# Layer 2 of the late blocks: half in parts, half plain, with the row moves, row loads and transposes reordered

## The reference, cut to what matters

```python
x = x + L0_xattn_ref(ctx_1024, _layernorm(x), ...)          # attention, 32 batches
def _L0_ffn_ref(...):                                        # D = 256, F = 1024, 8 experts
    assign = argmax(x @ centroids.T)                         # one expert for each token
    xn  = layer_norm(x) * ln_g[e] + ln_b[e]
    h   = relu(xn @ w1[e].T + b1[e])                         # layer 1: 256 -> 1024
    y   = x + h @ w2[e].T + b2[e]                            # layer 2: 1024 -> 256
    out = alpha * y + (1 - alpha) * x                        # alpha = sigmoid(x . centroid)
x = x + _L0_ffn_ref(_layernorm(x), ...)
```

## Time and profile before

| | us |
|---|---|
| median of 3 runs | 1070.32 (1070.15 to 1070.99) |
| the profiled execution | 1066.71 |
| its span | 1064.9 |
| TensorE matmul busy | 1051.3 (99%) |
| VectorE busy | 796.3 (75%) |
| ScalarE busy | 670.9 (63%) |
| GpSimd busy | 494.8 (46%) |

### The profile page before, as it was taken

The page is one execution under the profiler, slowest core; times in us unless marked ns, Lnnn a source line. Parts: engine busy times, 40 slices in busy tenths (PEclk is TensorE's granted clock), DMA queues, the critical chain, the costliest instruction groups (busy, mean ns, idle before and its releaser), DMA issues.

```text
span 1064.9 us, 24086 instructions
## 1 busy us (share of the span) xinstructions
PE 1051.3 (99%) x8454; PEld 941.1 (88%) x8454; DVE 796.3 (75%) x1907; ACT 670.9 (63%) x1820; POOL 494.8 (46%) x647
## 2 busy tenths in 40 slices
PE   8989999999999999999999999999999999999998
PEld 6879898988888888989898888888898999999997
DVE  7867888888888988888888888898886554544441
ACT  6765757585676766575757567676555646656551
POOL 2744464646454555546464645455445342222222
PEclk9999999999999999999999999999999999999999
DMA  6576667585757676766658575766367657767670
GB/s 209 120 194 148 165 166 189 139 218 139 207 144 185 150 194 163 188 161 174 181 146 213 145 206 139 190 149 157 90 170 226 236 196 249 240 223 232 227 260 28
DMA packets 159660, 190.51 MB, mean 179 GB/s; under 512 B 17453, under 2 KB 149037, under 8 KB 154672
## 3 DMA queue, kind: packets, MB, share of 16 engines
q1 hardware_dynamic: 155088, 179.09, 61.6%
q0 software_dynamic: 3360, 8.53, 2.2%
q10 hardware_dynamic: 1088, 1.31, 0.4%
HBM read 65.72 MB, written 46.07 MB: 105 GB/s over the span
## 4 chain that ended last, share of the span: by engine, by line
PE 94%; POOL 2%; DVE 2%; DMA 1%; issue 1%; ACT 0%; SPq 0%; POOLq 0%; DVEq 0%
PE psum L698 17%; PE psum L731 16%; PE psum L873 12%; PE psum L768 11%; PE psum L858 10%; PE psum L747 9%; PE psum L783 9%; PE psum L717 8%; PE psum L786 1%; POOL prob L1701 1%; POOL w_o_lo L1758 0%; DVE neg_max L1307 0%; DMA prob_t<-r_ring 0%; POOL r_ring L1701 0%; DMA c_in<-in_ctx_in 0%
## 5 line engine op out<-in xcount | busy, mean ns | idle before, releaser
L1701 POOL TENSOR_TENSOR prob<-prob,inv_sum 128x512 f32<-128x512 f32 x172 | 179.4, 1057 | 195.9 <-DVE inv_sum L1313 195.5
L1307 DVE TENSOR_REDUCE neg_max<-psum 128x2 f32<-128x512 f32 x256 | 162.2, 673 | 36.8 <-PE psum L747 36.8
L1052 ACT ACTIVATE prob<-psum,neg_max 128x256 f32<-128x256 f32 x344 | 160.4, 479 | 32.3 <-DVE neg_max L1307 31.7
L873 PE MATMUL psum<-w,v_n 128*128 128x256 f32 x608 | 134.2, 379 | 0.0
L1319 DVE STREAM_TRANSPOSE prob<-prob 128x512 f32<-128x512 f32 x172 | 118.5, 699 | 12.1 <-POOL prob L1701 11.7
L873 PEld LDWEIGHTS psum<-w,v_n 128*128 128x128 f32 x608 | 114.2, 190 | 14.8
L1701 POOL TENSOR_TENSOR w_ring<-w_ring,inv_sum 128x512 f32<-128x512 f32 x76 | 78.2, 1042 | 79.8 <-DVE inv_sum L1313 79.8
L1059 ACT ACTIVATE head_out_hi<-psum 128x512 fp32r<-128x512 f32 x52 | 31.0, 597 | 118.8 <-PE psum L768 103.0
L1775 POOL DMA_INDIRECT out<-x_in,r_ring x38 | 39.6, 1043 | 130.3 <-DVE x_in L1551 129.6
L1038 ACT ACTIVATE v_n<-psum 128x512 f32<-128x512 f32 x128 | 77.9, 609 | 27.4 <-PE psum L731 22.6
L1027 ACT ACTIVATE k_hi<-psum 128x512 fp32r<-128x512 f32 x128 | 77.1, 603 | 19.1 <-PE psum L698 17.8
(11 more groups left out here) (189 smaller groups left out, 2712.1 us busy)
## 6 DMA issues: line engine op xcount, KB each, us to landing
sorted_rows<-filler SPq DMA_DIRECT2D x54, 660.0 KB, 5.0
prob_t<-prob SPq DMA_DIRECT2D x172, 128.0 KB, 2.8
w_ring<-prob SPq DMA_DIRECT2D x172, 128.0 KB
w<-in_experts SPq DMA_DIRECT2D x19, 1024.0 KB
w_ring<-in_experts SPq DMA_DIRECT2D x18, 1024.0 KB, 5.9
prob_t<-w_ring SPq DMA_DIRECT2D x76, 128.0 KB, 2.8
w_ring<-w_ring SPq DMA_DIRECT2D x76, 128.0 KB
w_ring<-normed SPq DMA_DIRECT2D x56, 128.0 KB, 3.0
```

Source lines behind the costliest of these rows:

```text
L873: last = pe.matmul(bank[:, 0:d_model], hid[:, s % 2, f, i * P:(i + 1) * P], w2[:, f * d_model:(f + 1) * d_model], start=(f == 0), stop=(f ...
L1052: act.activation(prob_at(u, bb)[:, :, parity, i], scores_i, ACT.Exp, bias=neg_max[:, at, i:i + 1], accum_out=prob_sum[:, at, i:i + 1]).the ...
L1307: dve.tensor_reduce(neg_max[:, (4 * u + n) % 8, :], psum[:, n, :].rearrange("p (i j) -> p i j", i=2), AXIS_X, ALU.max, negate=True).then_i ...
L1701: pool.tensor_tensor(probs, probs, inverse, ALU.mult).then_inc(s_soft, 1)
```

## The change

For blocks from 4 on (`FIRST_SPLIT`), layer 2 takes the first four of its eight slices f in parts and the last four plain, both into the same PSUM bank. That needs high and low halves of the hidden layer and of w2 for those four slices:

- ScalarE's relu (`relu_parts`) writes slices 0 to 3 as float32 to `hid_raw` (one place), 4 to 7 to `hid_plain`; after gain and bias it rounds half of w2 (`high_weights_2`).
- VectorE splits the hidden slices (`split_hidden`: two casts and two subtractions of 128x512), between low w1 and the split of xn.
- GpSimd makes the low half of w2 (`low_weights_2`, 128x1024), between the base and the scatter.
- `finish` adds b2 directly into `fin`, since the place that it used is taken.

The order changes too. SyncE now runs for each s: move of the rows of s, vectors and rows of s + 1, w1 of s + 2, w2 and b2 of s. The wait for the block four back moves from `load_vectors` to `load_rows`. VectorE transposes the rows of s + 3, not s + 2, and does it after the split of xn and ahead of the finish of s.

```diff
@@ load_vectors / load_rows
-                    if s >= NR:
-                        sp.wait_ge(f_o, 2 * (s - NR) + 2)
-                        sp.wait_ge(f_out[(s - NR) % 2], 32 * ((s - NR) // 2 + 1))
+                    if s == NR:
+                        wait_read(sp, ("h", 3))
+                    elif s > NR:
+                        sp.wait_ge(f_ha, FC // 2 * (s - NR))
...
+                    elif s >= NR:
+                        sp.wait_ge(f_o, 2 * (s - NR) + 2)
+                        sp.wait_ge(f_out[(s - NR) % 2], 32 * ((s - NR) // 2 + 1))
@@ SyncE's loop
+                load_weights_2(n_early - 1)
+                load_b2(n_early - 1)
                 scattered(n_batches)
-                for s in range(n_early, n_slots + 1):
-                    run(s, (load_vectors,), (load_rows,), (load_weights_1,))
-                    run(s - 1, (load_weights_2,), (load_b2,))
+                run(n_early, (load_vectors,), (load_rows,), (load_weights_1,))
+                run(n_early + 1, (load_weights_1,))
+                for s in range(n_early, n_slots):
                     run(s, (move_rows,))
+                    run(s + 1, (load_vectors,), (load_rows,))
+                    run(s + 2, (load_weights_1,))
+                    run(s, (load_weights_2,), (load_b2,))
@@ TensorE
+                    def in_parts(bank, i, first):
+                        for n, (hw, hx) in enumerate(PASSES):
+                            for f in range(FS):
+                                last = pe.matmul(bank, hid_hl[hx][:, s % 2, f, i * P:(i + 1) * P], w2_hl[s % 2][hw][:, f, :], ...)
+                    def plain(bank, i, first):
+                        for f in range(FS, FC):
+                            last = pe.matmul(bank, hid_plain[:, s % 2, f - FS, i * P:(i + 1) * P],
+                                             w2_ring[s % NW2][:, f * d_model:(f + 1) * d_model], ...)
+                    bank = begin(("fy", s, 0))[:, 0:d_model]
+                    in_parts(bank, 0, True)
+                    plain(bank, 0, False).then_inc(f_y, 1)
+                    bank = begin(("fy", s, 1))[:, 0:d_model]
+                    plain(bank, 1, True)
+                    in_parts(bank, 1, False).then_inc(f_y, 1)
@@ ScalarE
+                def high_weights_2(s):
+                    act.wait_ge(f_w2[s % NW2], 16 * (s // NW2 + 1))
...
+                    act.activation(w2_hl[s % 2][0], w2_ring[s % NW2][:, 0:FS * d_model]..., ACT.Copy).then_inc(f_w2h, 1)
@@ VectorE
+                def split_hidden(s):
+                    for i in range(FS // 2):
+                        dve.wait_ge(f_ha, FC // 2 * (s - 1) + i + 1)
+                        if i == 0:
+                            wait_made(dve, ("fy", s - 2, 1))
+                        hi, lo = [h[:, s % 2, 2 * i:2 * i + 2, :].rearrange("p f t -> p (f t)") for h in hid_hl]
+                        then_next(dve.tensor_copy(hi, hid_raw[:, i, :]))
+                        dve.tensor_tensor(lo, hid_raw[:, i, :], hi, ALU.subtract).then_inc(f_hl, 1)
...
-                    run(s + 2, (transpose_rows,), (low_weights_1,), (split_xn,))
+                    run(s + 2, (low_weights_1,))
+                    run(s + 1, (split_hidden,))
+                    run(s + 2, (split_xn,))
+                    run(s + 3, (transpose_rows,))
                     run(s, (finish,))
@@ GpSimd
+                def low_weights_2(s):
+                    pool.wait_ge(f_w2h, s - FIRST_SPLIT + 1)
+                    raw = w2_ring[s % NW2][:, 0:FS * d_model].rearrange("p (f d) -> p f d", f=FS)
+                    pool.tensor_tensor(w2_hl[s % 2][1], raw, w2_hl[s % 2][0], ALU.subtract).then_inc(f_w2l, 1)
```

More of the change, by code:

```diff
@@ L179, in build @@
             k_s = [sbuf(a, f"k_{h}", [P, 2, 2, BANK], F32R) for h in ("hi", "lo")]
+            FS = FC // 2
+            with ExitStack() as late:
+                hid_hi = sbuf(late, "hid_hi", [P, 2, FS, BLOCK], F32R)
+                sbuf(late, "hid_between", [P, 3 * FS * BLOCK])
+                hid_lo = sbuf(late, "hid_lo", [P, 2, FS, BLOCK], F32R)
             v_n = sbuf(a, "v_n", [P, 2, 2, 2, BANK])
@@ L281, in build @@
             f_ha = sem("f_ha")
+            f_hl = sem("f_hl")
+            f_w2h = sem("f_w2h")
+            f_w2l = sem("f_w2l")
             f_y = sem("f_y")
@@ L306, in build @@
             hid = v_n[:].rearrange("p s a b n -> p s (a b n)").rearrange("p s (f t) -> p s f t", f=FC)
-            flat = "p b a h i s q -> p (b a h i s q)"
-            upd = prob_t_even[:].rearrange(flat)[:, 0:2 * d_model].rearrange("p (i d) -> p i d", i=2)
+            hid_hl = (hid_hi, hid_lo)
+            hid_raw = y_t[:].rearrange("p c b t -> p c (b t)")
+            hid_plain = prob_t_even[:].rearrange("p b a h i s q -> p b (a h i s q)").rearrange("p s (f t) -> p s f t", f=FC - FS)
+            w2_hl = [[w[:].rearrange(rule)[:, 0:FS * d_model].rearrange("p (f d) -> p f d", f=FS) for w in pair] for pair, rule in
+                     ((head_out, "p b c t -> p (b c t)"), (w_o, "p c n -> p (c n)"))]
             blocks = "p (j h i s k) -> p j h i s k"
@@ L876, in layer_2, with layer_2_split @@
                         last.then_inc(f_y, 1)
+                def layer_2_split(s):
+                    pe.wait_ge(f_w2h, s - FIRST_SPLIT + 1)
+                    pe.wait_ge(f_w2l, s - FIRST_SPLIT + 1)
+                    pe.wait_ge(f_hl, FS // 2 * (s - FIRST_SPLIT + 1))
+                    pe.wait_ge(f_ha, FC // 2 * s)
+                    def in_parts(bank, i, first):
+                        for n, (hw, hx) in enumerate(PASSES):
+                            for f in range(FS):
+                                last = pe.matmul(bank, hid_hl[hx][:, s % 2, f, i * P:(i + 1) * P], w2_hl[s % 2][hw][:, f, :],
+                                                 start=(first and n == 0 and f == 0), stop=(not first and n == 2 and f == FS - 1))
+                        return last
+                    def plain(bank, i, first):
+                        for f in range(FS, FC):
+                            last = pe.matmul(bank, hid_plain[:, s % 2, f - FS, i * P:(i + 1) * P],
+                                             w2_ring[s % NW2][:, f * d_model:(f + 1) * d_model],
+                                             start=(first and f == FS), stop=(not first and f == FC - 1))
+                        return last
+                    bank = begin(("fy", s, 0))[:, 0:d_model]
[4 more added lines that the diff above has]
+                    in_parts(bank, 1, False).then_inc(f_y, 1)
                 pe.wait_ge(s_blank, 1)
@@ L1543, in finish @@
                         wait_made(dve, item)
-                        last_reads(item, dve.tensor_tensor(upd[:, i, :], work_bank(number[item])[:, 0:d_model],
+                        if i == 0 and s >= 2:
+                            dve.wait_ge(f_out[s % 2], 32 * (s // 2))
+                        last_reads(item, dve.tensor_tensor(fin[:, s % 2, i, :], work_bank(number[item])[:, 0:d_model],
                                                           b2_ring[:, s % NR, :], ALU.add))
```

46 lines of the change are left out of this document (38 added, 8 removed).

## The result

The changed kernel takes 1076.73 us (median of five runs, 1075.95 to 1081.53), the kernel before, run beside it, 1070.37 us. The ratio is 1.0074, with a 95% interval of 1.0061 to 1.0087: slower, by 6.4 us. The profiled execution of after took 1075.95 us with a span of 1074.2 us. That is 9.2 us over the profiled execution of before, of which 1.8 us stand ahead of the late blocks already and are no part of the change: layer 2 of block 4 begins at 883.49 where before had 881.65, and the first such layer of the feed-forward part at 815.92 against 814.09. In after's trace the granted clock is 0.78, 0.50 and 0.87 in the three stretches of 2 us from 64 to 70 us, in the attention, and 1.00 there in before's; TensorE's time lost by it works out, as an estimate, at 2 x (0.22 + 0.50 + 0.13) = 1.7 us.

The account below looks back on a forecast made before the run. TensorE was taken to bound the kernel, at 99% busy; 8.7 us saved in layer 2 less a 5.5 us stall from a ring of waits gave 3.2 us less, 1067.1 us against 1070.3, range 1061.2 to 1075.

Parts of the forecast that it names:

- part 1: TensorE, layer 2: eight of 16 matmuls in parts save 0.58 us a block, 8.7 us over 15 blocks.
- T': TensorE's work per changed block, forecast at 12.08 us, against 12.66 us before.
- The ring: Finish, scatter, landing, row load, normalise, transpose, next finish: one turn per block, forecast 12.9 us, costing a 5.5 us stall.
- the landing: From the second scatter's end on GpSimd to SyncE's next issue: forecast 1.8 us.
- E: The end of a block's finish on VectorE (its last L1551), from which the turn's terms were added.
- The second scatter: On GpSimd: starts within VectorE's low w1, takes 2.76 us in place of 0.98, ends at E + 3.19.
- The lag at the start: How far block 4's finish ends behind the start of TensorE's next step: forecast 2.4 us.
- slack of 6.3: Lag the finish may have before TensorE waits: 12.08 less 5.8 us of VectorE work after E.
- L: Length of one turn from finish to finish: forecast 12.9 us, 0.8 us over T'.
- The third: Rival: hidden-split casts on VectorE also hold the scatter, turn 14.05 us, stall 18.7 us, 1080 us, slower; chance 0.20.
- The second: Rival: the scatter gets through, turn 11.9 us, no binding ring, all of part 1 gained, 1061.6 us; chance 0.22.
- The fourth: Rival: TensorE's records in parts are slower than in layer 1 or wait for a late half, 1066 to 1074 us; chance 0.08.

Follow-up runs that it names:

- e10: The changed kernel with VectorE's hidden split ahead of low w1, transpose still ahead of the finish: 1068.66 us, ratio to before 0.9992.
- e2: The changed kernel with the low half of w1 made for only 64 of 1024 columns from block 7 on: 1067.06 us, ratio to before 0.9976.
- e1: The changed kernel with VectorE's transpose of the rows of s + 3 behind the finish of s: 1064.51 us, ratio to before 0.9954.
- e9: As e1, with VectorE's hidden split ahead of low w1: 1061.61 us, ratio to before 0.9931.
- e3: The kernel before with layer 2 split in parts, but the old order on SyncE and VectorE: 1068.94 us, ratio to before 0.9985.
- e5: As e2, and only an eighth of w2 loaded from block 7 on: 1060.14 us, ratio to before 0.9915.
- e8: The changed kernel with only an eighth of w2 loaded from block 7 on: 1075.79 us, ratio to before 1.0054.
- e7: As e1, with SyncE sending w1 and w2 out ahead of the next rows: 1106.28 us, ratio to before 1.0342.
- e6: As e1, with ScalarE's high half of w2 made ahead of gain and bias: 1066.40 us, ratio to before 0.9973.

## Why the prediction was wrong

**What was right.** The bound and part 1: layer 2 is 6.33 us, T' = 12.08, 24 records 0.120 and 16 records 0.216 us apart. The ring: it is closed, it starts at block 4, the finish waits for the transpose, and TensorE is idle only from the steps after 938 us on. Its parts but one are near: the landing 1.3 us here and 1.8 forecast, from the rows' issue to the next E 6.9 against 7.2.

**The step that failed** is "The second scatter ... So it ends at E + 3.19". The sum had the first scatter start ahead of low w1 and go through, as in the earlier trace rows, and only the second held. In after low w1 waits for nothing at E, the first scatter starts 0.03 us behind it and is the one that is held, until E + 3.10; the second, 1.05 us, can only start then. The pair ends at E + 4.46, so this term alone was 1.27 us too small. (Only the scatters of blocks 4 and 5 have the forecast shape and end at E + 3.12 and E + 3.73.) That a scatter beside low w1 is held until 0.86 us after it was right: 0.89 here. The shorter landing and the shorter way from rows to finish took 0.55 to 0.7 us back. The turn came out at 13.61 in place of 12.9. Both ends of that term were in the earlier trace rows; what I took from them was which scatter is hit, and not what follows if it is the other.

**The lag at the start** was 1.66 us (891.48 - 889.82), not 2.4. The sum's formula with the measured numbers is 1.66 + 11 x (13.61 - 12.08) - 6.3 = 12.2 us without the 0.4, and 12.4 were lost by block 18's layer 1. So the way the stall was worked out holds, slack of 6.3 included; eleven turns made an error of 0.7 us in L into one of 7.8 us. That is more than the range had room for: it ended at L = 13.6 in name, but at 1075 us in time, where by its own formula L = 13.6 gives a stall of 13.2 and 1074.8 before anything else goes wrong.

**What was put at nothing** is the low half of w2 at the end. "The low w2 comes about 10 us ahead of its use, so I see no wait" was right as long as GpSimd isn't late. It is late at the ring's end, since the base waits for the landing of the scatter. That cost 2.08 + 0.62 = 2.7 us, and 0.25 us in the last layer 2: the difference between 12.4 and 15.4. It is the wait ahead of layer 2 that the prediction named as a sign of being wrong. The long turn alone turns the sign; the measured time lies above the range only with this term, since with the measured lag and turn the sum gives 1070.3 - 8.7 + 12.2 = 1073.8 us.

**The rivals.** The third had the sign right (slower from L = 13.2 on) and named the wrong cause: the casts of the hidden split don't keep the scatter waiting any longer. In after the held scatter ends 0.89 us after low w1 though a cast has begun, the next one takes 1.05 us while the split runs, and in e10 the two take 1.02 and 1.12. The second, that the scatter gets through, is refuted by the 3.15 us. The fourth holds only for that wait at the end. By the Trainium skill (SBUF — State Buffer, section Who interferes with whom) it should have been the other way round: subtractions harmless to GpSimd's making of descriptors, casts harmful. The runs disagree with the first half: a scatter takes 3.15 us beside a subtraction of 128x2048, and 1.15 us once that is cut to a sixteenth (e2). They don't refute the second: beside a cast of 128x512 the scatter of e10 takes 1.12 us and ends 0.85 us after the cast (997.98 against 997.13), as it does beside low w1. What is harmless here is the cast's 0.42 us; no scatter of these runs begins in a long one. Another rule of that section of the Trainium skill is that an operation of VectorE with two SBUF inputs and one of GpSimd that reads SBUF shut each other out. The trace of e1 agrees: the gated sum takes 2.10 us beside GpSimd's subtraction, against 0.48.

**Beyond the prediction.** The runs show the change to be sound in its first part, which two things then use up: the ring, and low w1 right behind the finish. Opening the ring (e1) is worth 12 us; freeing the scatter, 8 us with the ring closed (e10) and 2.9 more with it open (e9). Still open are why some loads of rows take longer (one with 4.49 us from the issue to the normalising made the turn of 14.94), and the shares of SyncE's moves and of the clock in e3's 4.4 us.

## What to carry to other kernels

When an order moves a step that waits for this block's transfers ahead of the step that starts them for the next one, it closes a ring; work out its turn against that of the bounding engine, and remember that an error in the turn counts once for every block. What follows an instruction at once on its engine decides what its consumers on the other engines meet: here a long subtraction right behind the finish cost 2 us on GpSimd in ten of twelve blocks, and four short instructions in between gave back all of it on GpSimd, though only a part in the turn (13.61 to 12.93 us). Cut suspects one at a time and together, since the second limit shows only when the first is gone (e2, e5 and e8).

## What the hardware did that was not expected

- A subtraction of 128x2048 on VectorE (2.29 us) holds an indirect DMA's issue on GpSimd until 0.85 to 0.90 us after its own end, even when the DMA's record starts only 0.03 us after it. The same distance stands behind short operations: 0.90 us after the 0.28 us of e2's narrow low w1, 0.85 us after a cast of 128x512 of 0.42 us (e10). Only their length makes them cheap, since a scatter that nothing holds takes about 1 us itself.
- What was first decides. A scatter whose record begins 0.03 us or more behind low w1's is held (3.15 us in after); at 0.01 and 0.02 us behind (e1 at 977.81, after at 891.42) it takes 0.98 and 1.02 us, and low w1 is drawn out to 2.34 and 2.35 us instead. 0.01 us between the records decides over 2.1 us.
- It goes both ways between other pairs: GpSimd's subtraction of 128x1024 (2.4 us) stretches VectorE's gated sum from 0.48 to 2.10 us (e1), and one of 2.54 us a subtraction of 128x512 from 0.69 to 2.73 us (e3).
- A scatter whose data go out beside the load of w2 lands later. From the end of its record to the next instruction on GpSimd are 2.2 to 4.0 us in e2 from block 7 on, and 1.6 to 2.8 us in e5, which differs only by loading one eighth of w2; at the end of after it is 5.3 us. Rows issued behind 2 MB were there after 6.25 us (e7), against 2.8.
- The granted clock fell to 0.50 behind single waits of TensorE of 3.31 us (e3) and 1.83 us (e10, where layer 1 at 1029.43 took 7.46 us in place of 5.98). Of the waits in the late blocks of after (up to 1.86 us) and e6 (up to 1.80 us) none had that behind it.
